# Three-stage weight quantisation: the block-scaling multiply on GpSimd, block scales two chunks ahead, four chunk buffers

## The chip, the cores and the metric

The kernel runs on one core of one Trainium2 chip. The metric is the device time of one execution in microseconds (us). An engine is named here by what it is: TensorE (PE in the rows), VectorE (DVE), ScalarE (ACT), GpSimd (POOL) and SyncE (SP), which issues the transfers of this kernel. All five have their own instruction queue and run it in order; between engines only semaphores set an order.

## What is computed

Two transformer-like layers on `x` (2 x 256 x 512), each of three parts with a layer norm in front and a residual around it. First layer: an attention by autocorrelation (the five best lags and lag 0 of each row), an 8-bit fake-quantised product with the context, and a feed-forward net in a block floating-point format. Second layer: attention with 32 heads over a paged cache, cross-attention with 16 heads, and a mixture of eight experts. The change is in the preparation of the feed-forward net's weights:

```
def _quant_elem(x, mbits):
    emin = 0.0
    max_norm = (2.0 - 2.0 ** (-mbits)) * 2.0 ** EMAX
    ax = jnp.abs(x)
    e = jnp.floor(jnp.log2(jnp.maximum(ax, 2.0 ** (-30))))
    e = jnp.maximum(e, emin)
    step = jnp.exp2(e - mbits)
    q = jnp.round(x / step) * step
    return jnp.clip(q, -max_norm, max_norm)

def _mx_quant(x, mbits):
    xb = x.reshape(s[:-1] + (s[-1] // BLOCK, BLOCK))
    amax = jnp.max(jnp.abs(xb), axis=-1, keepdims=True)
    shared_exp = jnp.floor(jnp.log2(jnp.where(amax > 0, amax, 1.0))) - EMAX
    scale = jnp.exp2(shared_exp)
    q = _quant_elem(xb / scale, mbits) * scale
...
    wq = _mx_quant(w, 1)     # blocks of 32, each with its own scale; w_gate, w_up, w_down
```

## The kernel before, in words

The weights of the feed-forward net are quantised once, at the start of the program, in 15 chunks: chunks 0 to 10 are two tiles of `wgu` (gate and up weights, 128 partitions x 1024 elements), chunks 11 to 14 one tile of `wd` (128 x 1408; `NCH` is 11). While that goes on, the same engines do the first attention (the Fourier transform, the search for the lags, the gathers and the sums of taps), quantise the context of the second part in four pieces, and compute the keys and values of the cross-attention from the context (`context_step`).

A chunk goes through these hands before the change:

1. SyncE loads it into one of two buffers (`WX`), once chunk c-2 has been read (`wx_used`).
2. VectorE, `weight_normalised(c)`: the largest magnitude of each block of 32 (L1021), its exponent, the scale and the inverse of the scale (L1023 to L1025), the weights times the inverse scale into another buffer (L1035), the exponent of each normalised weight (L1040).
3. ScalarE, `magic(c)`: a rounding constant for each weight from its exponent (L716).
4. VectorE, `weight_rounded(c)`: two operations that round (L1048, L1051), one that clips (L1052), into `WQ8`.
5. GpSimd, `scaled(c)`: times the block's scale (L581).
6. TensorE transposes the chunk (L1419), ScalarE copies it out of PSUM (L688, L694).

The order on each engine is written out by hand. VectorE takes `weight_normalised(c+1)` and then `weight_rounded(c)`; between them stand the search for the lags (L1095 to L1101, behind `weight_rounded(2)`) and the softmax of the taps (L1113, behind `weight_rounded(3)`). The scales lie in three buffers, so `weight_normalised(c)` for c of 3 and more waits until GpSimd has scaled chunk c-3 (`wq8_ready` at c-2). GpSimd has the four pieces of the context (L564, then L567 behind three operations of ScalarE, L723 to L727), the scalings and, from chunk 3 on, twenty gathers (L572, indirect transfers) in one queue. ScalarE takes `magic(c+2)`, the copy of chunk c, the copies of the context's keys and values, and the clipping of context piece c+2 in that order. TensorE takes the transposes of chunk c and then, for c of 0 and 2 to 8, two of the sixteen `context_step`s. SyncE issues its transfers in one row too: after chunk 7 it waits for the eighth `context_step` (`ectx_psum` at 8), loads the other half of the transposed context (L398), and only then chunk 8 and what follows. When the last chunk is rounded, VectorE adds the taps to `X` (L1123) and the second part begins.

Of the kernel before, what the change touches and what calls it, by code (L numbers as in the profile page):

```python
# [22 lines left out]
RT = TOK // P  # L23
# [32 lines left out]
def decoder_kernel(nc, x, ctx, ctx_t, qscale, wgu, wd, dft, idft, nyq, freqs, wq1, wk1, wv1, wo1,  # L56
                   kcache, vcache, block_idx, wq2, wk2, wv2, wo2, gate_w, expert_w, out):
    es = ExitStack()
    with es:
# [131 lines left out]
        WN2 = HT[:].rearrange("p k t -> p (k t)")[:, 0:IP]  # L191
# [5 lines left out]
        WX = at(49152, 2 * IP).rearrange("p (i n) -> p i n", i=2)  # L197
        WN = at(60416, IP)
        WM = at(66048, IP)
        WN1 = at(129216, IP)  # L200
# [67 lines left out]
        def bankb(n):  # L268
# [10 lines left out]
        names = """x_in qs_in dft_in freqs_in gw_in bidx_in ctxn_in ctxt_in ew_in wx_in0 wx_in1 kc_in vc_in  # L279
# [8 lines left out]
            wx_used wexp_ready magic_ready wq8_ready wt_psum wt_ev ectx_psum ectx_ev  # L288
# [24 lines left out]
        def weight_normal(c):  # L313
            n = CHUNKS[c]
            return (WN if c % 2 == 0 else WN1 if c < NCH else WN2)[:, 0:n]

# [41 lines left out]
        def _(sp):  # L358
# [4 lines left out]
            def load_chunk(c):  # L363
                if c >= 2:
                    sp.wait_ge(s["wx_used"], c - 1)
                dst = WX[:, c % 2, 0:CHUNKS[c]]
# [5 lines left out]
                sp.dma_start(dst, src).then_inc(s[f"wx_in{c % 2}"], 16)  # L372
# [158 lines left out]
        def _(pool):  # L531
# [43 lines left out]

            def scaled(c):
# [379 lines left out]
        def _(dve):  # L956
# [60 lines left out]
            def block_scale(src, n, down, blkinv=blkinv, blkscale=blkscale):  # L1017
# [7 lines left out]
                step(dve.reciprocal(blkinv[:, 0:nb], blkscale[:, 0:nb]))  # L1025

            def weight_normalised(c):

                n = CHUNKS[c]
                w, nn = WX[:, c % 2, 0:n], weight_normal(c)  # L1030
                dve.wait_ge(s[f"wx_in{c % 2}"], 16 * (c // 2 + 1))
                if c >= 3:
                    dve.wait_ge(s["wq8_ready"], c - 2)
                block_scale(w, n, 0.25, blkinvs[c % 3], blkscales[c % 3])
                dve.tensor_tensor(blocks(nn, n), blocks(w, n), spread(blkinvs[c % 3], n // MX), ALU.mult)\  # L1035
                   .then_inc(s["wx_used"], 1)
# [812 lines left out]
```

## Time and profile before

| | us |
|---|---|
| three runs: median (lowest, highest) | 1281.72 (1279.67, 1283.8) |
| the profiled execution | 1283.38 |
| its span | 1281.5 |
| TensorE busy | 1142.7 (89%) |
| VectorE busy | 907.3 (71%) |
| GpSimd busy | 522.0 (41%) |
| span until the taps are added | 169.24 |

The profile shows one execution. The span goes from its first instruction to its last; the execution's own time is 1.9 us more. Shares of busy time are means over the whole program, in which the two large attentions (from about 270 us on) keep TensorE full. The stage that the change touches is the first 169 us, and there the rows of single instructions tell more than the shares.

### The profile page before, as it was taken

How to read it: one execution, taken by the hardware profiler on the slowest of the kernel's cores; microseconds unless marked ns; L12 is line 12 of the kernel's file. 1: busy time of each engine (PE TensorE's matmuls, PEld its weight loads, DVE VectorE, ACT ScalarE, POOL GpSimd, SP SyncE). 2: the span in 40 equal slices, each digit the busy share in tenths (PEclk: the TensorE clock that was granted, in tenths of full speed). 3: DMA queues.
4: the chain of work that ended last, by engine and by line, in shares of the span. 5: the costliest groups of instructions: out<-in, count | busy, mean ns of one | idle time of the engine just before them, and what ended most of it. 6: DMA issues, size and time to landing. Idle time of an engine off the chain costs nothing.

```text
span 1281.5 us, 17687 instructions
## 1 busy us (share of the span) xinstructions
PE 1142.7 (89%) x5902; PEld 901.5 (70%) x5902; DVE 907.3 (71%) x1489; ACT 611.7 (48%) x1201; POOL 522.0 (41%) x380
## 2 busy tenths in 40 slices
PE   4778743768999999999999999979899999997998
PEld 2333321336688888888888888766798988886887
DVE  6988998887586868777777777654566666666344
ACT  3523423222565656565665666542565656553111
POOL 1374220010454655555555545441565555551000
PEclk9878865869999999999999999998999999998999
DMA  8245425011101010100101000140101010001121
GB/s 306 80 131 193 144 80 203 13 33 42 46 17 62 17 57 22 47 30 21 56 20 57 20 33 13 58 119 24 56 14 50 20 30 20 19 26 66 66 98 65
DMA packets 39332, 79.30 MB, mean 62 GB/s; under 512 B 9587, under 2 KB 20340, under 8 KB 36084
## 3 DMA queue, kind: packets, MB, share of 16 engines
q1 hardware_dynamic: 37684, 73.43, 17.2%
q0 software_dynamic: 1600, 5.24, 1.3%
q8 instruction: 28, 0.46, 0.1%
q14 instruction: 20, 0.16, 0.0%
HBM read 70.54 MB, written 10.22 MB: 63 GB/s over the span
## 4 chain that ended last, share of the span: by engine, by line
PE 73%; DVE 15%; ACT 4%; DMA 3%; issue 3%; POOL 1%; SPq 1%; ACTq 0%; DVEq 0%; POOLq 0%
PE PS L1532 20%; PE PS L1533 19%; PE PS L1534 19%; PE PS L1626 9%; DVE blkamax L1021 2%; PE PS L1398 1%; DVE arena L1051 1%; DMA arena<-ek_dram 1%; PE PS L1695 1%; ACT arena L825 1%; DMA cs<-in_freqs 1%; DVE arena L1035 1%; DMA arena<-in_wgu 1%; PE PS L1382 1%; DVE arena L1048 1%
## 5 line engine op out<-in xcount | busy, mean ns | idle before, releaser
L614 POOL TENSOR_TENSOR arena<-arena,rsum 128x768 f32<-128x768 f32 x192 | 281.9, 1469 | 412.8 <-DVE rsum L1207 412.8
L840 ACT ACTIVATE PTH<-PS 128x384 fp32r<-128x384 f32 x384 | 168.2, 490 | 255.6 <-PE PS L1626 255.4
L1202 DVE TENSOR_REDUCE nmax<-PS 128x1 f32<-128x768 f32 x192 | 183.0, 954 | 140.1 <-PE PS L1534 138.0
L1249 DVE TENSOR_TENSOR PTL<-PS,PTH 128x384 fp32r<-128x384 f32 x384 | 194.5, 548 | 4.3 <-ACT PTH L840 3.6
L825 ACT ACTIVATE arena<-PS,nmax 128x768 f32<-128x768 f32 x192 | 174.2, 907 | 24.8 <-DVE nmax L1202 24.3
L1626 PE MATMUL PS<-identf,arena 128*128 128x128 f32 x1152 | 158.4, 273 | 2.8 <-DVE PTL L1249 1.9
L1626 PEld LDWEIGHTS PS<-identf,arena 128*128 128x128 f32 x1152 | 129.9, 140 | 5.7 <-POOL arena L614 4.1
L1532 PE MATMUL PS<-PTH,VSH 128*128 128x512 f32 (+1 forms) x198 | 81.1, 410 | 2.5 <-DVE OTL L1223 2.0
L1532 PE MATMUL PS<-WOH,OTH 128*128 128x512 f32 (+1 forms) x192 | 79.5, 414 | 4.0 <-DVE OTL L1279 3.7
L601 POOL TENSOR_TENSOR WQL<-arena,WQH 128x512 fp32r<-128x512 f32 (+1 forms) x48 | 57.9, 1209 | 61.1 <-ACT WQH L673 61.1
L1532 PE MATMUL PS<-HTH,WQH 128*128 128x512 f32 (+1 forms) x192 | 80.3, 418 | 0.0
L1534 PE MATMUL PS<-WOH,OTL 128*128 128x512 f32 (+1 forms) x192 | 76.7, 400 | 0.0
L1534 PE MATMUL PS<-PTH,VSL 128*128 128x512 f32 (+1 forms) x198 | 76.6, 387 | 0.0
L1533 PE MATMUL PS<-WOL,OTH 128*128 128x512 f32 (+1 forms) x192 | 76.4, 398 | 0.0
L1533 PE MATMUL PS<-PTL,VSH 128*128 128x512 f32 (+1 forms) x198 | 75.8, 383 | 0.0
L1533 PE MATMUL PS<-HTL,WQH 128*128 128x512 f32 (+1 forms) x192 | 75.8, 395 | 0.0
L1534 PE MATMUL PS<-HTH,WQL 128*128 128x512 f32 (+1 forms) x192 | 75.6, 394 | 0.0
L1217 DVE TENSOR_TENSOR QTL<-arena,QTH 128x512 fp32r<-128x512 f32 (+1 forms) x40 | 67.8, 1694 | 10.6 <-ACT QTH L817 10.6
L1207 DVE RECIPROCAL rsum<-psum_exp 128x1 f32<-128x1 f32 x192 | 31.5, 164 | 59.7 <-ACT arena L825 53.1
L601 POOL TENSOR_TENSOR WOL<-arena,WOH 128x512 fp32r<-128x512 f32 (+1 forms) x48 | 70.8, 1475 | 0.0
L1532 PE MATMUL PS<-PTH,VH 128*96 128x256 f32 x192 | 56.0, 292 | 2.4 <-DVE OTL L1223 2.0
L1534 PE MATMUL PS<-PTH,VL 128*96 128x256 f32 x192 | 53.8, 280 | 0.0
(255 smaller groups left out, 2630.5 us busy)
## 6 DMA issues: line engine op xcount, KB each, us to landing
arena<-in_wq SPq DMA_DIRECT2D x32, 256.0 KB, 2.6
arena<-in_wo SPq DMA_DIRECT2D x8, 1024.0 KB, 4.8
arena<-in_expert_w SPq DMA_DIRECT2D x8, 1024.0 KB, 4.8
arena<-in_wgu SPq DMA_DIRECT2D x11, 512.0 KB
arena<-v_dram SPq DMA_DIRECT2D x8, 384.0 KB, 3.5
arena<-in_wq SPq DMA_DIRECT2D x16, 192.0 KB, 2.4
arena<-in_wo SPq DMA_DIRECT2D x4, 768.0 KB, 5.2
arena<-in_wd SPq DMA_DIRECT2D x4, 704.0 KB
```

The source lines that it names most:

```text
L601: pool.tensor_tensor(fr(lo), raw, hi, ALU.subtract).then_inc(s["w_ready"], 1)
L614: pool.tensor_tensor(PR[:, u % 4, :], PR[:, u % 4, :], rsum[:, u % 4:u % 4 + 1].broadcast_to([P, KEYS]), ALU.mult).then_inc(s["pn_ready"], 1)
L825: act.activation(PR[:, slot, :], SC[pair][:, 0:KEYS], ACT.Exp, bias=nmax[:, slot:slot + 1], accum_out=psum_exp[:, slot:slot + 1]).then_inc ...
L840: act.activation(fr(PTH[:, (u // 4) % 2, 3 * half:3 * half + 3, u % 4 * P:(u % 4 + 1) * P]), bank(B_PT[half])[:, 0:3 * P].rearrange("p (k ...
L1202: dve.tensor_reduce(nmax[:, slot:slot + 1], SC[pair][:, 0:KEYS], AX.X, ALU.max, negate=True)\
L1207: dve.reciprocal(rsum[:, slot:slot + 1], psum_exp[:, slot:slot + 1]).then_inc(s["rsum_ready"], 1)
L1217: dve.tensor_tensor(fr(QTL[0:hd, j, :]), QT[0:hd, j, :], QTH[0:hd, j, :], ALU.subtract)\
L1249: dve.tensor_tensor(fr(PTL[:, (u // 4) % 2, ks, cols]), bank(B_PT[half])[:, 0:3 * P].rearrange("p (k c) -> p k c", k=3), PTH[:, (u // 4) % ...
L1532: pe.matmul(out, fr(xh), fr(yh), start=start, stop=False)
L1533: pe.matmul(out, fr(xh), fr(yl), start=False, stop=False)
L1534: return pe.matmul(out, fr(xl), fr(yh), start=False, stop=stop)
L1626: mm = pe.transpose(bank(B_PT[half])[:, k * P:(k + 1) * P], PR[:, u % 4, c * P:(c + 1) * P], identf[:])
```

## The change

GpSimd now does the multiply by the inverse scale, in place in the chunk's own buffer (`normalised`); VectorE's step c is `weight_scale(c+2)`, `weight_exponent(c+1)`, `weight_rounded(c)`. There are four chunk buffers in place of two and three further tiles for the normalised weights, and a buffer is loaded again once its chunk c-4 is rounded (`wq_rounded`). The gathers go two ahead of each scaling in place of four. The wait for a free scale buffer has the same text, but now belongs to chunk c+2.

```diff
@@ load_chunk
-                if c >= 2:
-                    sp.wait_ge(s["wx_used"], c - 1)
-                dst = WX[:, c % 2, 0:CHUNKS[c]]
+                if c >= 4:
+                    sp.wait_ge(s["wq_rounded"], c - 3)
+                dst = weight_chunk(c)
@@ GpSimd
+            def normalised(c):
+                n = CHUNKS[c]
+                w = blocks(weight_chunk(c), n)
+                pool.wait_ge(s["inv_ready"], c + 1)
+                pool.tensor_tensor(w, w, spread(blkinvs[c % 3], n // MX), ALU.mult).then_inc(s["norm_ready"], 1)
...
             context_quantised(0)
+            normalised(0)
+            normalised(1)
             context_quantised(1)
             for c in range(3):
+                normalised(c + 2)
                 scaled(c)
                 if c < 2:
                     context_quantised(c + 2)
...
             for c in range(3, len(CHUNKS)):
-                for n in range(4 * (c - 3), min(4 * (c - 2), RT * LAGS)):
+                for n in range(2 * (c - 3), min(2 * (c - 2), RT * LAGS)):
                     gather(n)
+                if c + 2 < len(CHUNKS):
+                    normalised(c + 2)
                 scaled(c)
@@ VectorE
+            def weight_scale(c):
+                dve.wait_ge(s[f"wx_in{c % 4}"], 16 * (c // 4 + 1))
                 if c >= 3:
                     dve.wait_ge(s["wq8_ready"], c - 2)
+                block_scale(weight_chunk(c), CHUNKS[c], 0.25, blkinvs[c % 3], blkscales[c % 3], "inv_ready")
...
+            def weight_exponent(c):
+                n = CHUNKS[c]
+                dve.wait_ge(s["norm_ready"], c + 1)
                 if c:
                     dve.wait_ge(s["magic_ready"], c)
+                dve.tensor_scalar(WM[:, 0:n].bitcast(U32), weight_chunk(c).bitcast(U32), EXPONENT, None,
+                                  ALU.bitwise_and).then_inc(s["wexp_ready"], 1)
...
+            def weight_step(c):
+                if c + 2 < len(CHUNKS):
+                    weight_scale(c + 2)
+                if c + 1 < len(CHUNKS):
+                    weight_exponent(c + 1)
+                weight_rounded(c)
...
-            weight_normalised(0)
-            weight_normalised(1)
-            weight_rounded(0)
-            weight_normalised(2)
-            weight_rounded(1)
+            weight_scale(0)
+            weight_scale(1)
+            weight_exponent(0)
+            weight_step(0)
+            weight_step(1)
...
-            weight_normalised(3)
-            weight_rounded(2)
+            weight_step(2)
```

On VectorE one chunk in the middle of the stage reads like this before, in the order of its queue (`blkamax` holds the blocks' largest magnitudes, `arena` the chunks; in brackets the semaphores that an instruction waits for; `dve_chain` is VectorE's own):

```order
L1021 TENSOR_REDUCE blkamax<-arena 128x32 [waits wq8_ready,wx_in0]
L1023 TENSOR_SCALAR blkamax<-blkamax 128x32 [waits dve_chain]
L1024 TENSOR_SCALAR blkscale<-blkamax 128x32 [waits dve_chain]
L1025 RECIPROCAL blkinv<-blkscale 128x32 [waits dve_chain]
L1035 TENSOR_TENSOR arena<-arena,blkinv 128x1024 [waits dve_chain]
L1040 TENSOR_SCALAR arena<-arena 128x1024 [waits magic_ready,wx_used]
L1048 SCALAR_TENSOR_TENSOR arena<-arena 128x1024 [waits magic_ready]
L1051 SCALAR_TENSOR_TENSOR arena<-arena 128x1024 [waits wt_psum,dve_chain]
L1052 TENSOR_SCALAR arena<-arena 128x1024 [waits dve_chain]
```

and this after, here step 4, in which the first four rows are of chunk 6:

```order
L1029 TENSOR_REDUCE blkamax<-arena 128x32 [waits wq8_ready,wx_in2]
L1031 TENSOR_SCALAR blkamax<-blkamax 128x32 [waits dve_chain]
L1032 TENSOR_SCALAR blkscale<-blkamax 128x32 [waits dve_chain]
L1033 RECIPROCAL blkinv<-blkscale 128x32 [waits dve_chain]
L1052 TENSOR_SCALAR arena<-arena 128x1024 [waits magic_ready,norm_ready]
L1060 SCALAR_TENSOR_TENSOR arena<-arena 128x1024 [waits magic_ready]
L1063 SCALAR_TENSOR_TENSOR arena<-arena 128x1024 [waits wt_psum,dve_chain]
L1064 TENSOR_SCALAR arena<-arena 128x1024 [waits dve_chain]
```

The multiply is gone from VectorE's queue, the exponent is of chunk 5, the rounding of chunk 4, and the reduction's wait for `wq8_ready` is now for the scaling of chunk 3, whose rounding is the last row of the step before.

GpSimd's queue from the first piece of the context to the scaling of chunk 1, before (L564 and L567 are the context's pieces, L581 the scalings):

```order
L564 TENSOR_SCALAR arena<-arena,inv_s,qs 128x1024 [waits ctxn_in,qs_ready]
L567 TENSOR_SCALAR arena<-arena,qconst 128x1024 [waits cn_clipped]
L564 TENSOR_SCALAR arena<-arena,inv_s,qs 128x1024 [waits ctxn_in]
L567 TENSOR_SCALAR arena<-arena,qconst 128x1024 [waits cn_clipped]
L581 TENSOR_TENSOR arena<-arena,blkscale 128x1024 [waits wq_rounded]
L564 TENSOR_SCALAR arena<-arena,inv_s,qs 128x1024 [waits ctxn_in]
L567 TENSOR_SCALAR arena<-arena,qconst 128x1024 [waits cn_clipped]
L581 TENSOR_TENSOR arena<-arena 128x1024 [waits wq_rounded]
```

and after (L560 and L563 the context's pieces, L577 the new multiplies, L584 the scalings):

```order
L560 TENSOR_SCALAR arena<-arena,inv_s,qs 128x1024 [waits ctxn_in,qs_ready]
L563 TENSOR_SCALAR arena<-arena,qconst 128x1024 [waits cn_clipped]
L577 TENSOR_TENSOR arena<-arena,blkinv 128x1024 [waits inv_ready]
L577 TENSOR_TENSOR arena<-arena 128x1024 [waits inv_ready]
L560 TENSOR_SCALAR arena<-arena,inv_s,qs 128x1024 [waits ctxn_in]
L563 TENSOR_SCALAR arena<-arena,qconst 128x1024 [waits cn_clipped]
L577 TENSOR_TENSOR arena<-arena 128x1024 [waits inv_ready]
L584 TENSOR_TENSOR arena<-arena,blkscale 128x1024 [waits wq_rounded]
L560 TENSOR_SCALAR arena<-arena,inv_s,qs 128x1024 [waits ctxn_in]
L563 TENSOR_SCALAR arena<-arena,qconst 128x1024 [waits cn_clipped]
L577 TENSOR_TENSOR arena<-arena,blkinv 128x1024 [waits inv_ready]
L584 TENSOR_TENSOR arena<-arena 128x1024 [waits wq_rounded]
```

Four multiplies have come into this piece of the queue. The scaling of chunk 1 stays behind the third piece of the context, as before, and has the multiply of chunk 3 in front of it.

## Rows read from the trace of the kernel before

**Rows 1.** The page's head, and the chain that ended last by engine.

```profile
span 1281.5 us, 17687 instructions
...
PE 73%; DVE 15%; ACT 4%; DMA 3%; issue 3%; POOL 1%; SPq 1%; ACTq 0%; DVEq 0%; POOLq 0%
```

**Rows 2.** Busy time by stretch: us and instructions of PE, PEld, DVE, ACT, POOL.

```profile
104.66:169.24 64.58, 53.35 (x183) 25.32 (x181) 62.82 (x67) 28.33 (x49) 19.14 (x10) 0.92 0.38 129
```

**Rows 3.** Timeline of DVE (start us, us, instruction), one chunk of 1024, uncontended.

```profile
46.06 1.21 DVE L1021 TENSOR_REDUCE blkamax<-arena 128x32 f32<-128x1024 f32 x1
...
48.12 1.23 DVE L1035 TENSOR_TENSOR arena<-arena,blkinv 128x1024 f32<-128x1024 f32 x1
49.37 0.69 DVE L1040 TENSOR_SCALAR arena<-arena 128x1024 uint32<-128x1024 uint32 x1
49.98 1.22 DVE L1048 SCALAR_TENSOR_TENSOR arena<-arena 128x1024 f32<-128x1024 bf16 x1
```

**Rows 4.** Timeline of DVE and POOL, two places where both run.

```profile
39.07 2.34 POOL L581 TENSOR_TENSOR arena<-arena,blkscale 128x1024 bf16<-128x1024 bf16 x1
...
39.57 2.92 DVE L1048 SCALAR_TENSOR_TENSOR arena<-arena 128x1024 f32<-128x1024 bf16 x1
...
85.20 1.21 DVE L1021 TENSOR_REDUCE blkamax<-arena 128x32 f32<-128x1024 f32 x1
85.37 1.91 POOL L581 TENSOR_TENSOR arena<-arena 128x1024 bf16<-128x1024 bf16 x1 [5.32 <-DVE arena L1052]
...
86.45 0.87 DVE L1023 TENSOR_SCALAR blkamax<-blkamax 128x32 uint32<-128x32 uint32 x1
```

**Rows 5.** POOL by line and form: busy us, mean ns.

```profile
L614 POOL TENSOR_TENSOR arena<-arena,rsum 128x768 f32<-128x768 f32 x192 | 281.9, 1469 | 412.8 <-DVE rsum L1207 412.8
L645 POOL TENSOR_TENSOR WV2L<-arena,WV2H 128x1536 fp32r<-128x1536 f32 x1 | 3.5, 3458 | 6.8 <-DVE HTL L1014 6.8
```

**Rows 6.** Timeline of POOL and DVE around the search for lags.

```profile
52.84 0.42 DVE L1095 COPY arena<-PS 128x256 f32<-128x256 f32 x1
...
54.56 1.20 POOL L567 TENSOR_SCALAR arena<-arena,qconst 128x1024 bf16<-128x1024 f32 x1 [9.90 <-ACT arena L727]
55.73 1.91 POOL L581 TENSOR_TENSOR arena<-arena 128x1024 bf16<-128x1024 bf16 x1
...
64.21 1.21 DVE L1021 TENSOR_REDUCE blkamax<-arena 128x32 f32<-128x1024 f32 x1
```

**Rows 7.** Timeline of SP and DVE: the half context, chunk 8, the taps.

```profile
95.59 0.38 SPq L398 DMA_DIRECT2D arena<-in_ctx_t  x1
...
104.66 1.22 DVE L1021 TENSOR_REDUCE blkamax<-arena 128x32 f32<-128x1024 f32 x1 [4.10 <-DMA arena<-in_wgu]
...
111.67 1.21 DVE L1021 TENSOR_REDUCE blkamax<-arena 128x32 f32<-128x1024 f32 x1
119.15 1.21 DVE L1021 TENSOR_REDUCE blkamax<-arena 128x32 f32<-128x1024 f32 x1
...
169.24 2.47 DVE L1123 TENSOR_TENSOR X<-X,PS 128x512 f32<-128x512 f32 x4
```

**Rows 8.** Timeline of DVE and POOL, chunks of 1408.

```profile
134.78 1.61 DVE L1021 TENSOR_REDUCE blkamax<-arena 128x44 f32<-128x1408 f32 x1
136.42 0.47 DVE L1023 TENSOR_SCALAR blkamax<-blkamax 128x44 uint32<-128x44 uint32 x1
...
137.61 1.62 DVE L1035 TENSOR_TENSOR arena<-arena,blkinv 128x1408 f32<-128x1408 f32 x1
139.27 0.89 DVE L1040 TENSOR_SCALAR arena<-arena 128x1408 uint32<-128x1408 uint32 x1
140.08 1.62 DVE L1048 SCALAR_TENSOR_TENSOR HT<-arena,HT 128x1408 f32<-128x1408 bf16 x1
...
144.00 2.56 POOL L581 TENSOR_TENSOR arena<-arena 128x1408 bf16<-128x1408 bf16 x1 [7.14 <-DVE arena L1052]
...
163.24 1.62 DVE L1048 SCALAR_TENSOR_TENSOR arena<-arena 128x1408 f32<-128x1408 bf16 x1
```

More of the change, by code:

```diff
@@ L196, in decoder_kernel @@
         blkscales = (blkscale[:], blk2[:, 2], blk2[:, 3])
-        WX = at(49152, 2 * IP).rearrange("p (i n) -> p i n", i=2)
-        WN = at(60416, IP)
+        WX = [at(offset, IP) for offset in (49152, 49152 + 4 * IP, 60416, 129216)]
         WM = at(66048, IP)
-        WN1 = at(129216, IP)
         MAGIC_AT = ((129216 + 4 * IP, 129216 + 6 * IP), (77312, 77312 + 2 * IP))
@@ L287, in decoder_kernel @@
             qs_ready cn_used csum_psum csum_used q1_ready at_psum at_ready b_psum b_used
-            wx_used wexp_ready magic_ready wq8_ready wt_psum wt_ev ectx_psum ectx_ev
+            inv_ready norm_ready wexp_ready magic_ready wq8_ready wt_psum wt_ev ectx_psum ectx_ev
             hq_ready hqt_psum hqt_ready gu_psum tanh_ready up_used sg_free iq_ready iqt_psum iqt_ready
@@ L311, in decoder_kernel, with weight_chunk @@
         KPAIRS = KV1 // 2
-        def weight_normal(c):
-            n = CHUNKS[c]
-            return (WN if c % 2 == 0 else WN1 if c < NCH else WN2)[:, 0:n]
+        def weight_chunk(c):
+            return WX[c % 4][:, 0:CHUNKS[c]]
         def weight_magic(c):
@@ L1015, in transposed, with block_scale @@
                            .then_inc(s["ht_lo"], 1)
-            def block_scale(src, n, down, blkinv=blkinv, blkscale=blkscale):
+            def block_scale(src, n, down, blkinv=blkinv, blkscale=blkscale, signal=None):
                 nb = n // MX
@@ L1024, in block_scale @@
                 step(dve.tensor_scalar(blkscale[:, 0:nb], blkamax[:, 0:nb], TINY, down, ALU.max, ALU.mult))
[L1025 to L1031, printed above, removed]
+                inverse = dve.reciprocal(blkinv[:, 0:nb], blkscale[:, 0:nb])
+                if signal:
+                    inverse.then_inc(s[signal], 1)
+                else:
+                    step(inverse)
+            def weight_scale(c):
+                dve.wait_ge(s[f"wx_in{c % 4}"], 16 * (c // 4 + 1))
                 if c >= 3:
                     dve.wait_ge(s["wq8_ready"], c - 2)
-                block_scale(w, n, 0.25, blkinvs[c % 3], blkscales[c % 3])
-                dve.tensor_tensor(blocks(nn, n), blocks(w, n), spread(blkinvs[c % 3], n // MX), ALU.mult)\
-                   .then_inc(s["wx_used"], 1)
-                dve.wait_ge(s["wx_used"], c + 1)
+                block_scale(weight_chunk(c), CHUNKS[c], 0.25, blkinvs[c % 3], blkscales[c % 3], "inv_ready")
+            def weight_exponent(c):
+                n = CHUNKS[c]
+                dve.wait_ge(s["norm_ready"], c + 1)
                 if c:
                     dve.wait_ge(s["magic_ready"], c)
-                dve.tensor_scalar(WM[:, 0:n].bitcast(U32), nn.bitcast(U32), EXPONENT, None, ALU.bitwise_and)\
-                   .then_inc(s["wexp_ready"], 1)
+                dve.tensor_scalar(WM[:, 0:n].bitcast(U32), weight_chunk(c).bitcast(U32), EXPONENT, None,
+                                  ALU.bitwise_and).then_inc(s["wexp_ready"], 1)
             def weight_rounded(c):
                 n = CHUNKS[c]
-                nn, mm, q = weight_normal(c), weight_magic(c), WQ8[:, c % 2, 0:n]
+                nn, mm, q = weight_chunk(c), weight_magic(c), WQ8[:, c % 2, 0:n]
                 dve.wait_ge(s["magic_ready"], c + 1)
@@ L1109, in _ @@
                .then_inc(s["tap_diff"], 1)
-            weight_normalised(4)
-            weight_rounded(3)
+            weight_step(3)
             dve.wait_ge(s["tap_exp"], 1)
```

9 lines of the change are left out of this document (3 added, 6 removed).

## The prediction

> **What bounds the kernel now.** I read the page first, then the busy time by stretch, then the timelines of VectorE, GpSimd, ScalarE, TensorE and SyncE up to 170 us, and the groups of GpSimd by form. The chain that ended last lies on TensorE for 73% of the span and on VectorE for 15% [rows 1]; the 73% are the attentions, which the change leaves alone. The stage of the change ends at 169.24, when VectorE, done with the last chunk, adds the taps [rows 7]. From 104.66 to there VectorE is busy for 62.82 of 64.58 us [rows 2]: it sets the pace, and so a multiply taken off it looks like a gain. Before 104.66 it had sat idle for 4.10 us on the load of chunk 8, which SyncE issues right behind the half context at 95.59 [rows 7]. What comes after 169.24 hangs on the taps' sum, so I count any delay of that instruction in full.
>
> One undisturbed chunk of 1024 on VectorE: reduction to inverse scale, call it S, 48.12 - 46.06 = 2.06; the multiply 1.23; the exponent, E, 49.98 - 49.37 = 0.61; the rounding, R, from 49.98 to the next start at 52.84, 2.86, and 0.08 until its last instruction is out: 2.94 [rows 3, 6]. The same for 1408: S 137.61 - 134.78 = 2.83, less the 0.29 that the tiny L1023 there lost (0.47 against 0.18), 2.54; E 0.81; R 144.00 - 140.08 = 3.92 with the signal to GpSimd [rows 8]. The period is 119.15 - 111.67 = 7.48 [rows 7], though the parts make 6.84: the rest is lost to GpSimd.
>
> **The lock.** At 85.37 GpSimd starts a scaling of 1.91. VectorE's reduction, begun at 85.20, keeps its 1.21; the next instruction, 32 elements wide, takes 0.87 and ends at 87.32, just after the scaling does (87.28). At 39.57 the rounding operation L1048 takes 2.92 in place of 1.22, again until 1.2 after the end of GpSimd's instruction (41.41) [rows 3, 4]. So in this stage a GpSimd multiply and every VectorE operation with two inputs in SBUF, or of the fast one-input kind, run one after the other; only the reduction runs beside. The Trainium skill says the same (SBUF — State Buffer, "Who interferes with whom"): GpSimd shares a port pair with VectorE, taken whole, while a reduction never contends. By that rule, which speaks against this change, the moved multiply hides only beside a reduction or an idle VectorE, and the time is the 1314 below; if it hid, it would be the 1293 of rival (a). The trace agrees with the rule, in the rows just named.
>
> **What the multiply costs on GpSimd.** No row shows it (float32, one full input, one spread over blocks). Nearest: the bf16 scaling with the same spread input, 1.91 for 1024 and 2.56 for 1408 [rows 4, 8]; the float32 multiply by one value per row, 1.469 for 768 [rows 5], which lies on the line through these two (1.91 less 256 x 0.65 / 384, 1.48 at 768). I take 1.91 and 2.56. Above: two full float32 inputs, 3.458 for 1536, 2.25 ns an element, so 2.3 and 3.2 [rows 5]. Below: 0, if it ran unlocked beside VectorE. The Trainium skill gives a two-input float32 operation on GpSimd 4497 ns for 2048 elements (GPSIMD Engine Reference, "Elementwise — side-by-side cycle accounting"); by that the multiplies would be an estimated 2.2 and 3.1, and the total near my upper end. The rows with a broadcast input speak for less, so the sum stays with them.
>
> **The new wait.** VectorE's step c now starts with the scale of chunk c+2, which waits for `wq8_ready` at c, that is for the scaling of chunk c-1. That scaling starts when step c-1's last instruction ends. So VectorE stands idle for the whole scaling, where before the reduction ran beside it: P = 1.91 + 0.08 = 2.0 per chunk (2.64 at 1408). Queued behind the waiting reduction is everything else of VectorE: exponent, rounding, in step 2 the search for lags, and so ScalarE's constants and GpSimd's next scaling. Then S; GpSimd spends this time on its two gathers; E goes first, since VectorE is there already; then GpSimd's multiply takes the port, N = 2.0, and VectorE's first rounding operation waits for it; then R. A step of 1024 costs 2.0 + 2.06 + 0.61 + 2.0 + 2.94 = 9.6 against 7.48. Nothing in it runs beside anything.
>
> **The first part, to chunk 4.** The scaling of chunk 0 ended at 41.41 [rows 4]. The multiply of chunk 2 is queued right ahead of it; those of 0 and 1 delay the second piece of the context, but its load, which stood behind chunk 2's buffer, is about 2 us earlier. I take one multiply, +1.9; bounds 0 and +4. The third piece of the context follows TensorE's work behind that scaling, so L567, at 54.56 before [rows 6], comes at 56.5, then its 1.2, the multiply of chunk 3, the scaling of chunk 1: 61.5. VectorE's step 2 waits for just this. Before, that chunk's work began at 46.06 without a wait. From 61.5: S, E, R, 5.6, the search for lags starts at 67.1 (before 52.84); it takes 64.21 - 52.84 = 11.4 [rows 6], to 78.5. Step 3: S, E, N, R = 7.6 (its scaling is long over), to 86.1; scaling 2.0; step 4, 7.6: 95.7. So the scaling of chunk 4 starts at 95.8, before at 85.37 [rows 4].
>
> **Chunk 8.** From that scaling TensorE's transposes and two context steps lead to the half context's load and chunk 8: 104.66 - 85.37 = 19.3 [rows 4, 7]. Nothing in this is touched, so chunk 8 lands at 115.1. VectorE would be ready at 95.8 + 9.6 + 1.9 = 107.3: the idle time is about 8 in place of 4.10. Four buffers do not help, because the load waits for `ectx_psum`, not for a buffer. And VectorE now needs chunk 8 in step 6, with one chunk more still to be rounded than before.
>
> **From chunk 8 to the taps.** Step 6: 7.6 (the scaling before is over). 7 and 8: 9.6 each. 9 (scale and multiply of 1408): 2.0 + 2.54 + 0.61 + 2.64 + 2.94 = 10.7. 10 (exponent too): 10.9. 11 (rounding too): 2.0 + 2.54 + 0.81 + 2.64 + 3.9 = 11.9. 12 (scaling too): 12.5. 13 has no scale and no multiply, but the scaling of chunk 12 holds the port: 0.81 + 2.64 + 3.9 = 7.3. 14 as before, 169.24 - 163.24 = 6.0 [rows 7, 8]. Sum 86.1, against 169.24 - 104.66 = 64.6 before. The taps are added at 115.1 + 86.1 = 201.2, 32 later. Of the 32, 10.4 come from the first part and 21.5 from the second.
>
> Hidden at nothing: fewer gathers per scaling (each tap's gathers are still issued at least a step ahead of TensorE's use); ScalarE's constants (one step of slack); the copies of the key cache, issued when TensorE has the last tap, which move with the taps' sum (I estimate 3 us less lead before it, after the scaling of chunk 12 has moved back; if the second part waited for them, those 3).
>
> The profiled execution took 1283.38, its span 1281.5. 1283.4 + 32 = 1315.3; the median of the three runs lies 1.7 lower, so I forecast 1314 for a median, 2.5% slower.
>
> **Rivals.**
> (a) The multiply hides: float32 with an input spread over blocks does not exclude VectorE. Then 2.0 goes in steps 3, 4 and 6 to 8, 2.64 in steps 9 to 12: 20.6 less, 1293. For it: no row shows this very form. Against it: L1048, itself with a float32 output, stood still beside GpSimd's instruction [rows 4]. 10%.
> (b) Dearer: multiplies at 2.3 and 3.2 add 0.4 x 7 + 0.6 x 4 = 5; chunk 9, now issued together with chunk 8, may delay it by 2; four in front of the first scaling instead of 1.9 add 2. 1318 to 1323. For it: the 2.25 ns an element [rows 5]. 11%.
> (c) Not slower: VectorE keeps only its own S + E + R. This is decided by what the wait for the scaling and the locked multiply cost together in a chunk: below 7.48 - 5.6 = 1.9 the change gains. If both were free (the scaling done before VectorE asks, the multiply unlocked), the rest after chunk 8 would be 5.6 x 3 + 6.1 + 6.3 + 7.3 x 2 + 4.7 + 6.0 = 54.5 in place of 64.6, and with chunk 8 2 us earlier the time would be 1270. For it: VectorE is the busy engine [rows 2], and GpSimd has 45 of 64.6 us to spare. Against it: the wait alone is 2.0, since the scaling of chunk c-1 can't begin before step c-1 ends, and that order is in the two queues themselves. 4%.
>
> **How the numbers follow.** The forecast, its terms good to 11 or so either way by the bounds named at them, has 75%: 1303 to 1325. (a) has 10%, (b) 11% and lies within 1325, (c) 4%. From 1303 I let the range go down to 1297, for a multiply that hides in part. It then leaves out (a), (c) and, for terms that err in one direction, some 4 in 100. About 0.3%, 4 us, is what a measurement of this kernel can tell from no change: faster 3% and same 2%, both from (c) and from mixtures of (a) and (c), slower 95%.
>
> **What would show it.** In the profile after: VectorE's reduction idle before each chunk for about 2 us and released by GpSimd's scaling L584 (the wait right); L577 at 1.9 and 2.6 (the price right); L1060 of a step at about 3.1 in place of 1.22, or L577 long in its place (the lock right), where 1.22 beside a running L577 would speak for (a); L1114, the search for lags, at about 67; chunk 8's reduction at about 115, released by its load; the taps' sum at about 201. A taps' sum below 175 would make the prediction wrong altogether; one near 180 would be (a).

## The result, and the profile after

| | before | after |
|---|---|---|
| median of four runs (lowest, highest), us | 1282.76 (1279.67, 1285.0) | 1304.83 (1302.33, 1306.41) |
| profiled execution, its span | 1283.38, 1281.5 | 1302.33, 1300.5 |
| taps' sum in that profile | 169.24 | 194.45 |

The ratio is 1.0172, 95% interval 1.0153 to 1.019: slower, inside the range, 9 us under the forecast of 1314. In the chain that ended last VectorE's share went from 15 to 18% and TensorE's from 73 to 71% [rows 1]:

```profile
span 1300.5 us, 17687 instructions
...
PE 71%; DVE 18%; ACT 4%; DMA 2%; POOL 2%; issue 1%; SPq 1%; DVEq 0%; ACTq 0%
```

The busy times from chunk 8 to the taps' sum, to hold against the stretch of [rows 2] (columns: the stretch and its length; busy time and count of TensorE's matmuls, its weight loads, VectorE, ScalarE, GpSimd; granted clock; DMA share; GB/s):

```profile
110.09:194.45 84.36, 60.56 (x184) 28.42 (x182) 69.82 (x64) 30.96 (x52) 49.57 (x27) 0.84 0.39 124
```

The stretch is 84.36 long, not 64.58. VectorE has lost seven multiplies there (an estimated 10.2: 3 of 1.23, 4 of 1.62) and gained one exponent and one rounding, since the lead is longer (3.5), and yet is busy longer, 69.82 for 62.82: the time in which it stands still beside GpSimd counts as busy. And it is idle for 14.5 where it had been for 1.8. Which wait that is, the waits of VectorE from 22 to 190 us say (us in all, times, the longest):

```profile
DVE blkamax L1029 <- POOL arena L584: 33.9, 9, 11.7
...
DVE blkamax L1029 <- DMA arena<-in_wgu: 6.9, 1, 6.9
```

The first row is new: the reduction waits for a scaling nine times, 6.9 and 11.7 in the first part, and from chunk 7 on 2.09 six times and 2.74 once. Now the timeline of the kernel after, to hold against [rows 3, 4 and 7]. L1029 is the reduction, L1052 the exponent, L577 the new multiply, L1060, L1063 and L1064 the rounding, L584 the scaling, L1114 the search for lags, L394 the half context, L1139 the taps' sum:

```profile
59.92 1.22 DVE L1029 TENSOR_REDUCE blkamax<-arena 128x32 f32<-128x1024 f32 x1 [11.69 <-POOL arena L584]
65.27 0.42 DVE L1114 COPY arena<-PS 128x256 f32<-128x256 f32 x1
...
93.83 1.91 POOL L584 TENSOR_TENSOR arena<-arena 128x1024 bf16<-128x1024 bf16 x1 [2.88 <-DVE arena L1064]
...
103.35 0.38 SPq L394 DMA_DIRECT2D arena<-in_ctx_t  x1
...
110.09 1.22 DVE L1029 TENSOR_REDUCE blkamax<-arena 128x32 f32<-128x1024 f32 x1 [6.89 <-DMA arena<-in_wgu]
...
128.78 1.22 DVE L1029 TENSOR_REDUCE blkamax<-arena 128x32 f32<-128x1024 f32 x1 [2.09 <-POOL arena L584]
130.03 0.18 DVE L1031 TENSOR_SCALAR blkamax<-blkamax 128x32 uint32<-128x32 uint32 x1
...
130.46 0.35 DVE L1033 RECIPROCAL arena<-arena 128x32 f32<-128x32 f32 x1
130.74 0.84 DVE L1052 TENSOR_SCALAR arena<-arena 128x1024 uint32<-128x1024 uint32 x1
131.08 2.26 POOL L577 TENSOR_TENSOR arena<-arena 128x1024 f32<-128x1024 f32 x1
131.50 2.92 DVE L1060 SCALAR_TENSOR_TENSOR arena<-arena 128x1024 f32<-128x1024 bf16 x1
134.46 1.23 DVE L1063 SCALAR_TENSOR_TENSOR arena<-arena 128x1024 bf16<-128x1024 bf16 x1
135.72 0.43 DVE L1064 TENSOR_SCALAR arena<-arena 128x1024 bf16<-128x1024 bf16 x1
136.22 1.91 POOL L584 TENSOR_TENSOR arena<-arena 128x1024 bf16<-128x1024 bf16 x1 [2.88 <-DVE arena L1064]
138.24 1.62 DVE L1029 TENSOR_REDUCE blkamax<-arena 128x44 f32<-128x1408 f32 x1 [2.09 <-POOL arena L584]
...
194.45 2.47 DVE L1139 TENSOR_TENSOR X<-X,PS 128x512 f32<-128x512 f32 x4
```

From 128.78 on the reader sees one step of 9.46 us, in which no pass over a chunk is done beside another: reduction and scale (beside which GpSimd issues its two gathers), exponent, then GpSimd's multiply, behind which L1060 stands for 1.7 of its 2.92, the rest of the rounding, GpSimd's scaling, and the next reduction 0.11 after it. L577 shows 2.26 because it starts while L1052 is still running; alone it takes 1.91.

The taps' sum is 25.2 late, the span 19.0 and the medians 22.1. What follows the taps' sum took 1106.0 here and 1112.3 before, with the same instructions. In the fourteen profiles of this study, one of each kernel, this remainder lies anywhere from 1105.0 to 1112.3, with the kernel before at the top. That the 6 us between these two kernels are scatter and none of the change is likely but not shown: by the interval of the ratio the medians are 19.6 to 24.4 apart, so 25.2 lies just outside. A part of the difference can be seen in TensorE's granted clock (the last but two column), in two pairs of stretches with the same work on TensorE. Kernel before:

```profile
281.80:289.00 7.20, 6.20 (x21) 4.92 (x20) 3.79 (x6) 3.34 (x7) 0.00 (x0) 0.65 0.00 0
314.00:326.30 12.30, 9.93 (x27) 4.75 (x26) 4.72 (x9) 3.26 (x7) 2.89 (x2) 0.86 0.06 21
```

Kernel after:

```profile
306.80:312.20 5.40, 4.40 (x21) 3.59 (x20) 3.78 (x6) 3.22 (x7) 0.00 (x0) 0.88 0.00 0
337.60:348.00 10.40, 8.04 (x26) 4.01 (x25) 4.51 (x9) 3.07 (x6) 2.89 (x2) 1.00 0.07 25
```

A mean clock of 0.88 for 0.65 and of 1.00 for 0.86 gives back 1.8 and 1.9 us. So below the kernels are compared by their taps' sums first, and by times where these can tell. A taps' sum is that of one profile. How far it can be trusted, two kernels show that are alike up to their chunk 8 (four scale buffers and the multiply on VectorE, without and with chunk 8 first): they reach the same reduction at 87.65 and 86.60. Differences of 1 us between taps' sums are therefore not told from scatter.

### The profile page after: what moved, and what is told of

The parts are those of the page before. It is cut to its first block, busy times and chain, and to the rows that moved or that the text cites. A ratio compares the mean times of both kernels' runs of the same rounds, so it can differ in the third digit from the quotient of the medians.

```text
span 1300.5 us, 17687 instructions
## 1 busy us (share of the span) xinstructions
PE 1142.9 (88%) x5902; PEld 901.4 (69%) x5902; DVE 903.2 (69%) x1474; ACT 610.5 (47%) x1201; POOL 552.5 (42%) x395
## 3 DMA queue, kind: packets, MB, share of 16 engines
HBM read 70.54 MB, written 10.22 MB: 62 GB/s over the span
## 4 chain that ended last, share of the span: by engine, by line
PE 71%; DVE 18%; ACT 4%; DMA 2%; POOL 2%; issue 1%; SPq 1%; DVEq 0%; ACTq 0%
PE PS L1548 19%; PE PS L1549 19%; PE PS L1550 19%; PE PS L1642 9%; DVE arena L1060 3%; DVE blkamax L1029 2%; DVE arena L1063 2%; POOL arena L584 1%; DMA arena<-ek_dram 1%; ACT arena L833 1%; DMA cs<-in_freqs 1%; PE PS L1711 1%; DVE arena L1052 1%; PE PS L1414 1%; PE PS L1398 1%
## 5 line engine op out<-in xcount | busy, mean ns | idle before, releaser
L1435 PE MATMUL PS<-identb,arena 128*128 128x128 bf16 x132 | 13.9, 271 | 53.9 <-POOL arena L584 53.9
```

## The experiments

The theory: the wait of the next scale for the scaling (a matter of how many small scale buffers there are) and the multiply on the shared port both cost, and add up. The rivals: one of them is the whole cause; or the cause is the first part, or chunk 8.

**Four scale buffers.** The kernel after with a fourth pair of buffers for the scales, so that the scale of chunk c+2 waits for the scaling of chunk c-2.

```diff
-                if c >= 3:
-                    dve.wait_ge(s["wq8_ready"], c - 2)
+                if c >= 4:
+                    dve.wait_ge(s["wq8_ready"], c - 3)
...              (blkinvs[c % 3], blkscales[c % 3] become c % 4)
```

> The changed kernel with four scale buffers instead of three, so that the scale of chunk c+2 waits for the scaling of chunk c-2 and not of c-1. My theory (the wait is a term of its own): the reduction runs beside the scaling again, about 1.2 us less per step from step 3 on, the step at about 8.3 us in place of 9.46, and the idle time before the reductions L1029 (2.09 each) gone; in the first part step 2 still has to wait for the multiply of chunk 3 in its exponent, so only about 4 us come back there. The taps' sum at about 182 in place of 194.45, the whole about 12 us less than the changed kernel. Rival (the multiply's lock alone makes the loss, the wait only stands where the lock would): within 3 us of the changed kernel.

Measured: 1292.06, ratio 1.0091 (1.0058 to 1.0124), taps' sum 179.74, 14.7 before that of the kernel after. No reduction waits for a scaling any more. In the first part the wait has moved to the exponent, which waits for the multiply behind the context piece. One of VectorE's waits, and the timeline of a step:

```profile
DVE arena L1053 <- POOL arena L578: 12.1, 2, 9.2
```

```profile
115.16 1.21 DVE L1030 TENSOR_REDUCE blkamax<-arena 128x32 f32<-128x1024 f32 x1
115.32 1.91 POOL L585 TENSOR_TENSOR arena<-arena 128x1024 bf16<-128x1024 bf16 x1 [2.88 <-DVE arena L1065]
116.40 0.86 DVE L1032 TENSOR_SCALAR blkamax<-blkamax 128x32 uint32<-128x32 uint32 x1
...
118.33 1.21 DVE L1061 SCALAR_TENSOR_TENSOR arena<-arena 128x1024 f32<-128x1024 bf16 x1
119.58 1.23 DVE L1064 SCALAR_TENSOR_TENSOR arena<-arena 128x1024 bf16<-128x1024 bf16 x1
120.38 2.19 POOL L578 TENSOR_TENSOR arena<-arena 128x1024 f32<-128x1024 f32 x1
120.84 2.02 DVE L1065 TENSOR_SCALAR arena<-arena 128x1024 bf16<-128x1024 bf16 x1
122.78 1.21 DVE L1030 TENSOR_REDUCE blkamax<-arena 128x32 f32<-128x1024 f32 x1
```

The scaling runs beside the reduction again. The multiply, now behind scaling and gathers, meets the clipping L1065, which takes 2.02 in place of 0.43. The step is 7.62, not the 8.3 that I expected. The multiply hardly hid, since the clipping loses 1.6 where L1060 had lost 1.7. What I had put too low is the wait: without its 2.09 the step loses only 0.69 to the scaling (L1032, 0.87 for 0.18); and the exponent is back at 0.63. Of the 14.7, 2.0 come before chunk 8 (its reduction at 108.09 for 110.09) and 12.7 behind it.

**The multiply back on VectorE.** The kernel after, in all else as it is (scales two ahead, four chunk buffers, three scale buffers).

```diff
-            normalised(0)                 (and every other call of normalised, on GpSimd)
...
-                block_scale(weight_chunk(c), CHUNKS[c], 0.25, blkinvs[c % 3], blkscales[c % 3], "inv_ready")
+                block_scale(weight_chunk(c), n, 0.25, blkinvs[c % 3], blkscales[c % 3])
+                dve.tensor_tensor(w, w, spread(blkinvs[c % 3], n // MX), ALU.mult).then_inc(s["norm_ready"], 1)
```

> The changed kernel with the multiply by the inverse scale back on VectorE, in place, right behind the scale of the same chunk; two chunks ahead, four chunk buffers and the wait for the scaling stay. My theory: VectorE gets 1.25 more per step and loses the 1.7 for which the rounding L1060 stood still, so a step gets only about 0.45 shorter at 1024 and 0.7 at 1408; two multiplies less in front of the scalings of chunks 0 and 1 on GpSimd bring about 3 us. The taps' sum at about 187, the whole about 7 us less than the changed kernel, still some 15 above the kernel before. Rival (the multiply on GpSimd is the whole cause): the time of the kernel before, within 4 us.

Measured: 1298.85, ratio 1.0142 (1.0117 to 1.0167), taps' sum 187.89. Only 6.6 of the 25.2 come back: the multiply's place is not the whole cause. The steps are 8.85, the reduction waits 2.09 as before.

**Hardly any multiply on GpSimd.** `normalised` multiplies only the first block of 32 of each row; the rest of the normalisation is left out.

```diff
+                w = weight_chunk(c)[:, 0:MX].rearrange("p (b e) -> p b e", e=MX)
-                pool.tensor_tensor(w, w, spread(blkinvs[c % 3], n // MX), ALU.mult)
+                pool.tensor_tensor(w, w, spread(blkinvs[c % 3], 1), ALU.mult)
```

> The changed kernel with GpSimd's multiply cut to the first block of 32 in each row; the rest of the normalisation is left out. My theory: 1.7 less per step of 1024 in which L1060 stood still, 2.36 for 1408, and about 3.5 in the first part: the taps' sum at about 173, the whole about 21 us below the changed kernel, near the kernel before. Rival (a) of the prediction (the multiply is hidden beside VectorE): within 4 us of the changed kernel.

Measured: 1282.04, ratio 1.0006 (0.9992 to 1.002), taps' sum 170.92 (I expected 173). One row of the timeline and one of VectorE's waits:

```profile
118.94 1.25 DVE L1061 SCALAR_TENSOR_TENSOR arena<-arena 128x1024 f32<-128x1024 bf16 x1
```

```profile
DVE blkamax L1030 <- POOL arena L585: 28.1, 9, 7.6
```

Without the multiply the rounding operation is back at 1.25, so the multiply alone had stretched it to 2.92. The wait for the scaling stands, 28.1 us, and only a kernel with a part of its work left out is level with the one before.

**Four scale buffers and the multiply on VectorE.** Both edits above together: what is left of the change is the lead of two chunks, the four chunk buffers and the gathers' spacing.

> The changed kernel with both terms taken away: the multiply on VectorE and four scale buffers; the queue orders and loads of the changed kernel stay. It is the fourth corner of a square with the changed kernel (taps' sum 194.45), four scale buffers alone (179.74) and the multiply back alone (187.89). My theory: the wait is the larger part and the lock the smaller, and the multiply's part shrinks once GpSimd can scale beside the reduction: taps' sum at 168 to 172, the step at about 7.3. Rival (the two costs simply add, 14.7 + 6.6): 173 or more.

Measured: 1285.59, ratio 1.0027 (1.0015 to 1.0039), taps' sum 174.79; not the 168 to 172 that I expected. The steps are 7.35, a little below the 7.48 of before. What is lost lies around one wait, to hold against the 4.10 of [rows 7]:

```profile
DVE blkamax L1025 <- DMA arena<-in_wgu: 11.1, 1, 11.1
DVE tapm L1129 <- ACT tapw L755: 5.8, 1, 5.8
```

Chunk 8's reduction comes 1.5 later than before (106.14 for 104.66; the half context is issued 2.8 later, at 98.36), and the stretch from there to the taps' sum is 4.1 longer, because one chunk more is still to be rounded in it.

With these four kernels the 25.2 can be told apart; that the three parts add up to it is so by construction:

| edit | taps' sum | worth |
|---|---|---|
| after | 194.45 | |
| a fourth scale buffer | 179.74 | 14.7 |
| and the multiply on VectorE | 174.79 | 5.0 |
| and the rest (lead of two, chunk buffers, gathers' spacing) undone: before | 169.24 | 5.5 |

In the other order the multiply is worth 6.6 and the buffer 13.1.

**Is the 5.5 chunk 8?** The same kernel, with chunk 8 loaded ahead of the half context.

```diff
-            for c in range(5, 8):
+            for c in range(5, 9):
                 load_chunk(c)
             sp.wait_ge(s["ectx_psum"], 8)
```

> The kernel of e11 (multiply on VectorE, four scale buffers, two chunks ahead) with chunk 8 loaded ahead of the wait for the eighth context step. e11 still adds the taps at 174.79, 5.5 us after the kernel before, and VectorE waits 11.1 for chunk 8 there against 4.10 before. My theory: that is the third part of the loss, the lead of two chunks asking for chunk 8 a step earlier; with the load in front all 11 us go: taps' sum at 163 to 166, below the kernel before. Rival (the lead costs otherwise, and the wait moves to another chunk or to ScalarE): 169 or later.

Measured: 1277.74, ratio 0.997 (0.9961 to 0.998), taps' sum 166.34, 8.5 less than without this edit and just outside the 163 to 166 that I expected; 1.1 of the 8.5 are there before the load can matter (86.60 for 87.65, above). VectorE's waits:

```profile
DVE tapm L1129 <- ACT tapw L755: 5.2, 1, 5.2
DVE blkamax L1025 <- DMA arena<-in_wgu: 3.6, 1, 3.6
```

The wait of 11.1 for chunk 8 is gone. The 3.6 are a new wait, for chunk 9 (its reduction at 105.03), which now stands right behind the half context; so my "all 11 us go" was wrong and a part of the rival was right. The kernel is 0.8 ahead of the next one, in which the same is done to the kernel before, which is to say level with it. So the lead of two costs nothing on balance; the 5.5 hang on chunk 8, asked for one step earlier and loaded no earlier.

**The kernel before with chunk 8 first.** The same edit.

> The kernel before with one change on SyncE: chunk 8 is loaded ahead of the wait for the eighth context step and the half context. My theory: VectorE's 4.10 us of waiting for chunk 8 was the load standing behind ectx_psum, and all comes back: the taps' sum at about 165 in place of 169.24, the whole 4 us less than before. Rival (the copies into the same memory crowd each other, or the wait only moves to a later chunk or to TensorE's half context): under 1.5 us less.

Measured: 1277.86, ratio 0.9966 (0.9948 to 0.9983), taps' sum 167.16. The wait of 4.10 is gone, but only 2.1 arrive at the taps' sum, not the 4 that I expected: the step from 108.52 to 117.06 is 8.54 long, with a wait of 0.8 for ScalarE's constant in it, and the ones ahead of it, four gathers in each, are 7.79.

**The order in the first part.** The kernel after, with the scalings of chunks 1 and 2 in GpSimd's queue ahead of the third and fourth piece of the context.

```diff
-                if c < 2:
-                    context_quantised(c + 2)
+                if c >= 1:
+                    context_quantised(c + 1)
```

> The changed kernel with GpSimd's queue changed in the first part: the multiply of chunk 3 and the scaling of chunk 1 ahead of the third piece of the context, those of chunks 4 and 2 ahead of the fourth. My theory: VectorE's wait of 11.69 before step 2 is the scaling of chunk 1 standing behind the context piece; it goes down to about 2, the search for lags starts at about 54 in place of 65.3, the scaling of chunk 4 at about 83 in place of 93.8, and all after it moves along: the taps' sum at about 184, 10 us less. Rival (the first part is bound by the chain of context pieces, ScalarE and TensorE up to the eighth context step, and VectorE's wait hides in it): chunk 8's reduction at 107 or later in place of 110.09, under 4 us less in all.

Measured: 1296.29, ratio 1.0114 (1.0093 to 1.0135), taps' sum 186.47, 8.0 earlier than after. Two rows, of VectorE and of GpSimd:

```profile
48.78 2.29 POOL L584 TENSOR_TENSOR arena<-arena 128x1024 bf16<-128x1024 bf16 x1 [2.88 <-DVE arena L1064]
...
51.54 1.21 DVE L1029 TENSOR_REDUCE blkamax<-arena 128x32 f32<-128x1024 f32 x1
```

The reduction of step 2 starts at 51.54 in place of 59.92: its longest wait (11.7) was for a scaling that stood behind a piece of the context in the queue, as the prediction had it. The search for lags comes at 57.77, not at the 54 that I expected, and the taps' sum 2.5 after the 184. The 8.0 all lie before chunk 8 (its reduction at 102.10 for 110.09), where the fourth scale buffer brought 2.0 of its 14.7; so the two overlap by 2.0 at most. The same order put on a kernel with four scale buffers, the multiply on VectorE and chunk 8 first still brings 7.5 (166.34 to 158.84, below).

**Chunk 8 first and this order, in the kernel before.**

> The kernel of e5 with GpSimd's scalings of chunks 1 and 2 also put ahead of the third and the fourth piece of the context. My theory: the exponential of the taps no longer waits for a scaling that stands behind the context, so VectorE's 4.98 us before the softmax of the taps go too; the taps' sum at about 160, the whole about 9 us less than before. Rival (the context chain is as long in the other order and comes out at its end): as e5, or slower than it.

Measured: 1273.65, ratio 0.9945 (0.9924 to 0.9965), taps' sum 162.00. The wait of 5.3 ahead of the softmax of the taps, which the kernel with chunk 8 first still had, is gone, as expected, though the taps' sum is 2 later than the 160 that I expected.

**All that helps, with the lead of two.** The kernel after, with the multiply on VectorE, four scale buffers, this order, and chunk 8 first.

> What of the change could be worth having, together: two chunks ahead, four chunk buffers, four scale buffers, the multiply back on VectorE, GpSimd's scalings of chunks 1 and 2 ahead of the context pieces, chunk 8 loaded ahead of the half context. My theory: with the multiply on VectorE and no wait for the scaling a step is the same 7.5 us as before, so running two ahead gains nothing over e6: within 3 us of it, about 9 us below the kernel before. Rival (the third stage of slack is worth something by itself): over 3 us better than e6.

Measured: 1270.18, ratio 0.991 (0.9889 to 0.9931), taps' sum 158.84. It beats both kernels, by 12 us the one before and by 34 us the one after. Over the last kernel, which has the same order and load but the structure of before, it gains 3.2 at the taps' sum, a little more than the 3 at which I had set the bound, so by my own bound the rival has it; but the intervals of the two ratios just overlap.

**How much of that is the gathers.** The kernel before with chunk 8 first and the new order, and two gathers per scaling for four.

```diff
-                for n in range(4 * (c - 3), min(4 * (c - 2), RT * LAGS)):
+                for n in range(2 * (c - 3), min(2 * (c - 2), RT * LAGS)):
```

> The kernel of e6 (chunk 8 loaded first, scalings ahead of the context pieces) with two gathers ahead of each scaling in place of four. e7 came out 3.2 us ahead of e6 at the taps' sum; it differs from e6 by two chunks of lead and by the gathers' spacing. My theory: GpSimd's gathers delay its scalings, and the spacing is what e7 gained: within 1 us of e7 at the taps' sum (158.84), about 3 us below e6. Rival (the lead of two chunks): within 1 us of e6 (162.00).

Measured: 1272.19, ratio 0.9926 (0.9909 to 0.9943), taps' sum 160.96. I had expected the spacing to be all of the 3.2. It gives 1.0 of them (its steps are 7.47 for 7.79), the lead of two the other 2.1 (steps of 7.20 to 7.50). By the taps' sums alone the 1.0 would be within the scatter; the steps show it.

**The gathers in the kernel before.** The same edit there, to see whether they hold up the load of chunk 8.

> The kernel before with two gathers ahead of each scaling in place of four. Chunk 8 landed 9.1 us after the half context was issued in the kernel before and 6.7 us in the changed one. My theory: the gathers' transfers share the memory with it, and two less in that stretch give those 2.4 us: chunk 8's reduction at about 102.3 in place of 104.66, the whole about 2 us less. Rival (the landing differs for another reason): chunk 8's reduction within 0.7 us of 104.66.

Measured: 1279.44, ratio 0.998 (0.9966 to 0.9994), taps' sum 168.51; chunk 8's reduction at 104.15 in place of 104.66. My 102.3 fell: the load lands 8.6 after the issue of the half context in this kernel and 9.1 in the one before [rows 7], but 6.7 in the kernel after, and the number of gathers ahead of a scaling accounts for 0.4 of that. What the profiles show instead is how much data of gathers is moved while the half context and chunk 8 are under way. Of each kernel that loads chunk 8 behind the half context:

| kernel | from the issue of the half context to chunk 8's reduction, us | moved by the gathers' queue in that time, MB |
|---|---|---|
| before | 9.07 | 0.82 |
| two gathers in the kernel before | 8.64 | 0.56 |
| four scale buffers and the multiply on VectorE | 7.78 | 0.52 |
| after | 6.74 | 0.12 |
| four scale buffers | 6.64 | 0.11 |
| multiply back on VectorE | 6.75 | 0.00 |
| hardly any multiply | 6.84 | 0.14 |
| new order | 6.71 | none |
| memset (the next one) | 6.66 | none |

A gather is 0.26 MB. In the kernel after, GpSimd issues none from 98.1 to 105.3; in the one before it issues six from 95.2 to 104.4. The 0.70 MB between these two kernels are an estimated 2.3 us at the 301 GB/s that this stretch has in the mean, for the 2.3 measured. So my theory may well have named the right cause and the wrong edit: two gathers per scaling took only 0.26 MB out of the stretch. No run was made for this alone.

**Which part of the multiply stops VectorE.** The kernel after, with GpSimd's multiply replaced by a memset, which only writes, of the same tile; the normalisation is left out and the weights are overwritten.

```diff
-                pool.tensor_tensor(w, w, spread(blkinvs[c % 3], n // MX), ALU.mult)
+                pool.memset(weight_chunk(c), 1.0)
```

> The changed kernel with GpSimd's multiply replaced by a memset of the same chunk, which reads nothing; the normalisation is left out and the weights are overwritten. Theory of a lock on reads (a GpSimd instruction that only writes does not stop a VectorE operation with two inputs): L1060 right behind the exponent at 1.22 even where it overlaps the memset. Rival (any GpSimd instruction on this memory stops VectorE): L1060 longer than 1.22 by what is left of the memset.

Measured, one execution: 1284.64, taps' sum 175.16. Timeline, with a memset of 1024 and one of 1408:

```profile
112.82 1.85 DVE L1052 TENSOR_SCALAR arena<-arena 128x1024 uint32<-128x1024 uint32 x1
113.15 0.97 POOL L577 MEMSET arena<- 128x1024 f32 x1
...
131.05 0.63 DVE L1052 TENSOR_SCALAR arena<-arena 128x1024 uint32<-128x1024 uint32 x1
131.20 1.70 POOL L577 MEMSET arena<- 128x1408 f32 x1 [0.53 <-DVE arena L1033]
131.60 1.21 DVE L1060 SCALAR_TENSOR_TENSOR arena<-arena 128x1024 f32<-128x1024 bf16 x1
```

The rounding operation with two inputs keeps its 1.21 beside the memset, where it took 2.92 beside the multiply. The exponent, with one input and one output, doesn't: 1.85 for 0.63, until 0.55 after the memset's end (a gather's issue ends at 113.15, just as the memset starts; in the kernel after, beside such an issue alone, it took 0.84). So in these rows it is GpSimd's reading that stops the two-input form, and its writing is enough to stop the fast one-input form.

## Why the prediction was right, point by point

- *The new wait, P = 2.0.* Right, and shown by taking it away: 2.09 before a chunk (2.74 where the scaling is of 1408), gone with a fourth scale buffer. This small buffer, and not the four large ones, set the lead; it is the largest part, 14.7 (or 13.1) of the 25.2, nearly all of it behind chunk 8 (12.7).
- *The multiply's price, N = 2.0.* Right: 1.91 where it runs alone, at 25.29, 37.72 and 56.04 in the trace, as I had taken from the scaling. 1408 elements came out at 2.87 to 3.08 with the wait for the exponent in it, for 2.64. By the Trainium skill's figure (GPSIMD Engine Reference, "Elementwise — side-by-side cycle accounting") it would have been an estimated 2.2; the trace says 1.91, and by it the sum stood. That the second input, spread over blocks, is what makes it cheaper than two full ones (2.25 ns an element [rows 5], for 1.87) is likely, but no run changed that alone.
- *The lock.* Right: L1060 at 2.92 beside the multiply, 1.25 without it, 1.21 beside a memset. Rival (a) falls by these. The rule of the Trainium skill (SBUF — State Buffer, "Who interferes with whom") agrees with these rows. Rival (b), a dearer multiply, falls by the 1.91; rival (c), not slower, by the result, and its point of decision stands: where both costs of a step were taken away (steps of 7.20 to 7.50) and chunk 8 came early, the kernel was faster than before. But there the multiply was back on VectorE; a multiply on GpSimd that stops nothing, as (c) had it, no run shows.
- *The step, 9.6.* 9.46 measured. The multiply cost VectorE 1.7 and not 2.0, because GpSimd starts it while the exponent still runs; the exponent, beside a gather's issue, cost 0.2 more. At 1408 elements L1060 lost 2.36 for 2.64.
- *The first part.* Search for lags 65.27 (I said 67.1), scaling of chunk 4 at 93.83 (95.8): 1.8 and 2.0 too late. The step that failed is the 1.9 that I gave to the multiply of chunk 2 ahead of the scaling of chunk 0, chosen between the bounds 0 and 4; measured, it was 0.1. GpSimd's timeline of the kernel before, to which the scaling at 39.07 belongs [rows 4], and of the kernel after:

```profile
36.95 2.15 POOL L567 TENSOR_SCALAR arena<-arena,qconst 128x1024 bf16<-128x1024 f32 x1 [3.65 <-ACT arena L727]
```

```profile
36.56 1.20 POOL L563 TENSOR_SCALAR arena<-arena,qconst 128x1024 bf16<-128x1024 f32 x1 [5.23 <-ACT arena L735]
37.72 1.91 POOL L577 TENSOR_TENSOR arena<-arena 128x1024 f32<-128x1024 f32 x1
39.59 1.91 POOL L584 TENSOR_TENSOR arena<-arena,blkscale 128x1024 bf16<-128x1024 bf16 x1
```

  The scaling ends at 41.50, where it had ended at 41.41 [rows 4]. The context piece ahead of it starts only 0.4 earlier; the rest of the multiply's 1.9 is paid for by VectorE, which from 34.7 to 41.6 stands waiting in the new kernel, so that the piece takes 1.20 for 2.15 and the scaling 1.91 for 2.34. I had priced GpSimd's work as if it still ran against VectorE. That the scaling of chunk 1 behind a piece of the context holds up step 2 is shown by the reordered queue, which moved that step by 8.4.
- *Chunk 8.* I took over the 19.3 of before from the scaling of chunk 4 to the landing; it was 16.3. The half context left 9.52 after the scaling (before 10.22) and chunk 8 was there 6.74 after that (before 9.07): 3.0 too much. This is the largest mis-sized term. I had written that nothing in this is touched, and had put the gathers' new spacing at nothing; but with it, and with the longer steps, hardly a gather's data is moved while chunk 8 is loaded, 0.12 MB for 0.82, and the load lands 2.3 sooner. That the one makes the other is what nine profiles agree on, not what a run of its own shows. VectorE's idle time behind the scaling of chunk 5, for which I had 8, was 4.9 (from 105.2 to 110.1; with the scaling 6.9), 2.9 less, for the same reason.
- *From chunk 8 to the taps.* 84.36 for 86.1; 1.7 too much: step 6 took 7.1 for 7.6, step 13 6.9 for 7.3, the others up to 0.2 less each.
- *Hidden at nothing.* Two gathers for four were worth 0.7 in the kernel before and 1.0 in the one reordered, both within the scatter of a taps' sum, though the ratio of 0.998 (0.9966 to 0.9994) says that the first is not nothing. The first copy of the key cache was issued 0.4 before the taps' sum for 3.9, a lead 3.5 shorter where I had 3; the remainder of the span was no longer for it.

By place the loss is 5.4 up to chunk 8 (I had 10.4) and 19.8 from there (21.5). The three terms (2.0, 3.0 and 1.7) make 201.2 - 194.45 = 6.7 with the rounding. The other 2.4 of the 9.2 between 1314 and 1304.83 lie outside the taps' sum, in the remainder, which the prediction took as fixed and which scatters by 7 us over the profiles. All three err the same way: the mechanism is right and the sum is too high throughout.

What I had not seen: I had written that VectorE needs chunk 8 one step sooner, and had counted that wait, but not that nearly all that the lead of two costs (5.5) hangs on that load, nor that with the two other costs gone and chunk 8 first the same lead makes the fastest kernel here.

## What to carry to other kernels

Before work is moved to GpSimd to relieve a busy VectorE, look at what runs beside it: here a multiply of 1.91 on GpSimd took 1.6 to 1.7 from a VectorE that had needed 1.23 for it, while the scaling, beside a reduction, took only 0.7. Each further chunk of lead needs one more of every buffer that the chunk holds to its end, the small ones (scales) as well as the large; the wait left in place with the same number becomes a wait for the last step. And a longer lead asks for each load earlier, so look at what the load itself waits for, and at what else is being moved meanwhile, before counting the gain.

## What the runs showed of the hardware

- A GpSimd memset (0.97 for 1024 float32, 128 partitions) lets a VectorE operation with two SBUF inputs run at its 1.21, but holds up a fast one-input operation (1.85 for 0.63).
- Beside a gather's issue on GpSimd (0.94) the exponent took 0.84 for 0.63, in the step shown above; the reduction of 1024 was never slower than 1.22 in any of these profiles.
- The same load of 128 x 1024 float32 behind the same half context lands 6.6 to 6.8 us after that one's issue in the six kernels in which 0 to 0.14 MB of gathers are moved meanwhile, and after 7.8, 8.6 and 9.1 in the three with 0.52, 0.56 and 0.82 MB. That the gathers' data are the cause is argued from these figures; no run was made to separate it.
- The part of the program behind the taps' sum, unchanged in its instructions, differs by 7 us over the profiles of fourteen kernels, in part with TensorE's granted clock (0.65 against 0.88 in one stretch). Executions of the kernel before differ by 9 us (1277.53 to 1286.59 in one set of 24).
